# Attention result turned in 32x32 blocks on VectorE instead of transposed on TensorE, and the query and key weights loaded between the pieces of x

## The reference, cut to what matters

```python
xn = _layernorm(x)                       # x: (2, 1024, 256)
# attention: 16 heads of width 16, causal
q = einsum('btc,hcd->bhtd', xn, Wq) + bq;  k, v alike
probs = softmax(q @ k^T * 16**-0.5 + causal)
y = (probs @ v).transpose(0, 2, 1, 3).reshape(B, T, 256)
attn = y @ Wo + bo
# experts: 8, each token goes to its top 2
logits = xn @ Wr;  top2, softmax over the two
h_e = (clip(silu(xn @ Wg[e]), -7, 7) * (xn @ Wu[e])) @ Wd[e]
out = x + attn + sum over the two chosen e of gate * h_e
```

## Time and profile before

| | before |
|---|---|
| median of 3 runs | 441.28 us (441.12 to 441.63) |
| span of the profiled execution, first to last instruction | 440.0 us |
| around the span: median less span | 1.28 us |
| granted TensorE clock, mean over the span | 0.984 |
| busy: PE / DVE / ACT / POOL | 422.0 / 314.2 / 237.6 / 194.6 us |

### The profile page before, as it was taken

One profiled execution on the slowest core, in us unless ns is written; L12 is line 12 of the kernel. 1 busy time (PEld: TensorE's weight loads), 2 busy tenths in 40 slices (PEclk: granted clock), 3 DMA queues, 4 the chain that ended last, 5 costly groups with the idle time before them and its releaser, 6 DMA issues.

```text
span 440.0 us, 8430 instructions
## 1 busy us (share of the span) xinstructions
PE 422.0 (96%) x2851; PEld 255.2 (58%) x2851; DVE 314.2 (71%) x1019; ACT 237.6 (54%) x551; POOL 194.6 (44%) x223
## 2 busy tenths in 40 slices
PE   8898979989999999999999999999999999999896
PEld 8486425656364366557666676565655664756333
DVE  6827999999888835885577735867576768591485
ACT  1563363433647665655564546646555547464992
POOL 5331256585054277346744256233743365212410
PEclk9999959998999999999999999999999999999999
DMA  7289896788076249435784069621893454110582
GB/s 237 70 218 201 277 207 182 257 280 269 4 150 181 83 135 230 154 118 187 184 233 175 23 187 221 189 87 50 245 256 107 145 155 153 21 38 3 169 310 97
DMA packets 40373, 71.34 MB, mean 162 GB/s; under 512 B 5893, under 2 KB 30598, under 8 KB 40332
## 3 DMA queue, kind: packets, MB, share of 16 engines
q0 software_dynamic: 9360, 39.99, 28.8%
q1 hardware_dynamic: 27132, 26.76, 24.5%
q10 hardware_dynamic: 3840, 4.08, 3.6%
HBM read 55.85 MB, written 15.60 MB: 162 GB/s over the span
## 4 chain that ended last, share of the span: by engine, by line
PE 72%; DVE 18%; issue 3%; DMA 3%; POOL 2%; ACT 1%; SPq 0%; ACTq 0%
PE psum L1364 15%; PE psum L1307 14%; PE psum L1268 11%; PE psum L1287 11%; PE psum L1373 7%; DVE psum L1004 5%; DVE mxa L1007 5%; PE psum L1223 3%; PE psum L1199 3%; PE psum L1347 2%; DMA bqk<-in_bqk 2%; PE psum L1316 2%; PE psum L1354 2%; DVE resid L976 1%; POOL probs L823 1%
## 5 line engine op out<-in xcount | busy, mean ns | idle before, releaser
L896 ACT ACTIVATE probs<-psum 128x512 f32<-128x512 f32 (+1 forms) x320 | 151.5, 575 | 38.6 <-PE psum L1287 37.8
L1004 DVE CUSTOM_DVE_ANT_0 psum<-psum,maskrow 128x128 f32<-128x128 f32 (+3 forms) x256 | 121.4, 505 | 18.1 <-PE psum L1268 17.8
L1268 PE MATMUL psum<-packk,packq 96*128 96x512 bf16 (+3 forms) x384 | 93.3, 328 | 2.5 <-DVE mxa L1004 1.2
L1007 DVE TENSOR_REDUCE mxa<-psum 128x1 f32<-128x512 f32 x128 | 87.7, 685 | 9.4 <-PE psum L1268 9.2
L1287 PE MATMUL psum<-packq,packk 99*128 99x512 bf16 (+3 forms) x384 | 90.5, 332 | 2.9 <-ACT probs L896 2.7
L1307 PE MATMUL psum<-probs,v 128*32 128x512 f32 (+3 forms) x768 | 76.1, 502 | 2.2 <-POOL probs L823 1.8
L823 POOL TENSOR_SCALAR_AFFINE_SELECT probs<-probs 128x512 f32<-128x512 f32 (+1 forms) x48 | 40.0, 836 | 64.1 <-ACT probs L896 63.6
L1268 PEld LDWEIGHTS psum<-packk,packq 96*128 96x128 bf16 x384 | 34.5, 97 | 54.7 <-issue 16.8
L1287 PEld LDWEIGHTS psum<-packq,packk 99*128 99x128 bf16 x384 | 33.0, 98 | 45.1 <-issue 12.7
L790 POOL DMA_INDIRECT xg<-xn_rows,token x39 | 37.6, 965 | 45.9 <-PE psum L1354 35.9
L1166 DVE SCALAR_TENSOR_TENSOR tanh<-tanh,psum 128x256 f32<-128x256 f32 x39 | 16.3, 417 | 49.8 <-ACT tanh L931 49.5
(11 more groups left out here) (127 smaller groups left out, 477.2 us busy)
## 6 DMA issues: line engine op xcount, KB each, us to landing
qk_parts<-stage SPq DMA_DIRECT2D x24, 256.0 KB, 2.9
stage<-expert_rows SPq DMA_DIRECT2D x16, 256.0 KB, 4.1
packq<-qk_parts SPq DMA_DIRECT2D x16, 192.0 KB, 4.6
packk<-qk_parts SPq DMA_DIRECT2D x14, 192.0 KB, 6.1
x<-in_x SPq DMA_DIRECT2D x4, 512.0 KB, 5.3
packq<-qk_parts SPq DMA_DIRECT2D x16, 128.0 KB, 6.2
xn_rows<-probs ACTq DMA_DIRECT2D x4, 512.0 KB, 14.5
out<-x SPq DMA_DIRECT2D x16, 128.0 KB, 2.5
```

The costliest lines, as they stand in the source:

```text
L896: act.activation(probs[:, g % RING, h, 0:width], psum[:, bank, 0:width], ACT.Exp, scale=SCALE)\
L1004: ins = dve.tensor_tensor_reduce(out=chunk, in0=chunk, in1=maskrow[:, BANK - width:], scale=1.0, scalar=NEG, op0=ALU.add, op1=ALU.max, acc ...
L1007: ins = dve.tensor_reduce(into, chunk, op=ALU.max, axis=AX.X)
L1268: pe.matmul(psum[:, bank, 0:width], packq[0:MAXROW, u % SLOTS, i // HALF, h, P * (i % HALF):P * (i % HALF + 1)], packk[0:MAXROW, u % SLOTS ...
```

## The change

Two edits in one, with the plan made anew from them.

**The end of a half without TensorE.** DVE transposes the bank of `pv` in 32x32 blocks straight from PSUM to SBUF (`turn`). Block (h, b) holds head h and 32 tokens, so after it each partition is a token of one head, 16 values and the sum beside them. `normalise` takes the reciprocal and multiplies from SBUF to SBUF, into one half of the 32 columns of `ynorm`: even units into the first 16, odd units into the last 16. When both units of a pair are in, a second block transpose (`turn_back`) writes `yt` in the layout that the projection wants, with the features in another order, and `wo` and `bv` are laid out in that order on loading. The transposes of `y` on PE and the copies on ACT (`copy_y`, `copy_yt`, `copy_yt_half`) are gone. `ynorm` of the second half lies in the memory of `wvr`, free once the v tiles are done; the hot rows of the routing lie in `yt` now, and the widened v bias in the first slot of `xgt`, so the first gather waits for the bias product.

**The loads at the start.** SP issues x piece 0 and 1, then `wqk`, then x piece 2 and 3, then the value weights, `bv`, `wo`, `bo`. ACT issues only the bias `bqk`, without a wait, on a semaphore of its own, which ACT's first `hi` waits for in place of PE. The first matmul of a query/key tile waits only for the first 128 features of its piece. `WARM` is 52, not 60.

```diff
-WARM = 60
+WARM = 52
...
-        job("SP", ("x", q), 500, lag=2000, due=-10, size=524288)
-    job("ACT", ("weights_qk",), 950, [("SP", ("x", 1))], due=-50, lag=2000, size=540000)
-    job("ACT", ("weights_v",), 2200, [("ACT", ("weights_qk",))], due=-50, lag=2000, size=820000)
+        job("SP", ("x", q), 500, lag=2000, due=q - 10, size=524288)
+    job("SP", ("weights_qk",), 500, due=-8.5, lag=2000, size=524288)
+    job("ACT", ("bias_qk",), 2000, due=-60, lag=2000)
+    job("SP", ("weights_v",), 2000, due=-5, lag=2000, size=820000)
...
-            pe(("xnt", q, c), 436, [("DVE", ("ln", q))], due=10 * q, takes=("xnt", q, c))
+            pe(("xnt", q, c), 436, [("DVE", ("ln", q))], due=10 * q if q > 1 else q, takes=("xnt", q, c))
...
-        after = [("ACT", ("xnt", 2 * b + n, c)) for c in range(DC)] + [("ACT", ("weights_qk",))]
-        pe(("qk1", k), 853, after, due=due, takes=("qk", k))
-        pe(("qk2", k), 853, [("PE", ("qk1", k))], due=due - 1)
+        after = [("ACT", ("xnt", 2 * b + n, 0)), ("SP", ("weights_qk",))]
+        pe(("qk1", k), 853, after, due=due, takes=("qk", k), lag=0)
+        pe(("qk2", k), 853, [("PE", ("qk1", k)), ("ACT", ("xnt", 2 * b + n, 1))], due=due - 1)
...
-            job("ACT", ("y", u, c), 465, after, due - 1000, frees=("y", u, c))
-            pe(("y_t", u, c), 450, [("ACT", ("y", u, c))], due, ("y_t", u, c))
...
-            dve(("norm", u, c), 626, after, due, ("y_t", u, c))
+            dve(("turn", u, c), 640, [("PE", ("pv", g))], due - 1000, ("y", u, c))
+            dve(("norm", u, c), 900, [("DVE", ("turn", u, c)), ("PE", ("v", NT - 1))], due - 1000)
+            if u % 2:
+                after = [("DVE", ("norm", u - 1, c)), ("DVE", ("norm", u, c))]
+                if u == 1:
+                    after += [("PE", ("list",))]
+                if u > G:
+                    after += [("PE", ("proj", HALF * c + HALF - 1))]
+                dve(("back", u, c), 640, after, due)
...
-                    pe(("proj_t", t), 220 if t < LATE else 110, [("DVE", ("norm", u, c))], pdue, ("proj_t", t))
...
-                    job("ACT", ("yt", t), 252 if t < LATE else 200, after, pdue, frees=("proj_t", t))
-                    pe(("proj", t), 853 if t < LATE else 427, [("ACT", ("yt", t))], pdue, ("proj", t))
+                    pe(("proj", t), 853 if t < LATE else 427, [("DVE", ("back", u, c))], pdue, ("proj", t))
...
+            def turn(u, c):
+                bank = wait_filled(dve, ("y", u, c))
+                if u == c == 0:
+                    dve.wait_ge(ones_in, 16)
+                dve.transpose(yturn[:, :, :].rearrange("p a b -> p (a b)"), psum[:, bank, :]).then_inc(freed[bank], 1)
+
             def normalise(u, c):
-                bank = wait_filled(dve, ("y_t", u, c))
-                part = psum[:, bank, :].rearrange("p (t h w) -> p t h w", t=4, h=UH)
-                chain(rec_ready, dve.reciprocal(rec[:, :, :], part[:, :, :, HD]))
...
-                dve.tensor_tensor(dst, part[:, :, :, 0:HD], rec[:, :, :].unsqueeze(3).to_broadcast([P, 4, UH, HD]),
-                                  ALU.mult).then_inc(freed[bank], 1)
+                wait_freed(dve, ("y", u, c))
+                chain(rec_ready, dve.reciprocal(rec[:, :], yturn[:, :, HD]))
+                at = HD * (u % 2)
...
+                dve.tensor_tensor(ynorm[c][:, :, at:at + HD], yturn[:, :, 0:HD],
+                                  rec[:, :].unsqueeze(2).to_broadcast([P, BANK // QUAD, HD]), ALU.mult).then_inc(y_normal, 1)
+
+            def turn_back(u, c):
...
+                dve.wait_ge(y_normal, normals_before(u, c))
+                dve.transpose(yt[:, u % G // 2, BANK * c:BANK * (c + 1)],
+                              ynorm[c][:, :, :].rearrange("p a b -> p (a b)")).then_inc(y_back, 1)
...
+            def head_rows(t, c):
+                if t % HALF == 0:
+                    pe.wait_ge(y_back, backs_before(t, c))
+                return yt[:, c, P * (t % TB):P * (t % TB + 1)]
...
-            def transpose_y(u, c):
-            def transpose_heads(t):
-            def transpose_first_heads(t):
...
+    def head_order(w):
+        return np.moveaxis(w.reshape(DC, 2, UH, HD, -1), (2, 1, 3, 0), (0, 1, 2, 3)).reshape(P, DC, -1)
```

142 lines of the change are left out of this document (57 added, 85 removed).

## The result

The changed kernel takes 445.85 us (median of 4 runs, 445.62 to 446.2) against 441.45 us for the kernel before on the same chip: a ratio of 1.0086, 95% interval 1.0062 to 1.0109. It is slower, where I forecast 432.1 us. The profiled execution spans 443.9 us against 440.0, so 13.1 us are missing from the forecast span of 430.8. The other 0.6 us lie around the span (445.85 - 443.9 = 1.95, where I had put 1.3).

The account below looks back on a forecast made before the run. PE was taken as the bound from 120 to 400 us and DVE from 42 to 110. Terms -2.4 + 0.9 - 8.7 + 1.0 = -9.2 gave a span of 430.8, plus 1.3 makes 432.1 us; range 427.0 to 438.0.

Parts of the forecast that it names:

- the start: Loading and first query/key product: earlier bias and weights start it at 11.5 to 11.6 us, carried on; -2.4 us.
- the stretches that PE bounds: 120 to 432 us: 9.9 us of PE transposes go, 1.2 us of waits come back; -8.7 us.
- that row as a rival: ACT's queue stands 4.18 us in a DMA issue at 36.24; the start's gain is swallowed, 434.5 us; chance 0.11.
- The stretch that DVE bounds: 42 to 110 us: one block transpose, 0.65 us, and normalisations held by POOL, 0.25 us; +0.9 us.
- the 1.2 us put down for all waits together: 120 to 432 us: PE waits from 17 us more DVE work, taken against the 9.9 us removed.
- 0.25 us on 16: Each of 16 normalisations, now with both inputs in SBUF, held by POOL for 0.25 us on average.
- PE busy for 98% from 120 to 400 us: Sign for the PE-bound term: PE still busy 98% or more there, unit ends drifting ahead 1.2 us per unit.
- The end: After the last `pv`: expert sums before the reciprocal make the end 7.2 us instead of 6.2; +1.0 us.
- The rivals: PE work back as waits, 435.8 (0.20); start swallowed, 434.5 (0.11); more off, 428.5 (0.08); DVE the bound, 452 (0.05).
- The one on the slow side: DVE becomes the bound through 1.37 us block transposes and 0.8 us holds; 452 us with half exposed; chance 0.05.

Follow-up runs that it names:

- both_dues: The changed kernel with the due times and releases of the first transposes and query/key products as before; 441.45 us.
- load_dues: The kernel before with the start edit's loads, but the first transposes' and query/key products' due times and releases as before; 440.7 us.
- turn_only: The changed kernel with the start taken back (weights behind piece 1 on ACT's queue, 60 warming transposes), only the attention edit left; 440.66 us.
- load_only: The kernel before with the start edit alone (loads moved, bias apart, 52 warming transposes, second feature chunk awaited later); 445.63 us.
- light_before: The kernel before, order unchanged, with one PE transpose of each attention result instead of four; 439.34 us.
- rec_order: rec_psum's order of all engines, with the reciprocals in SBUF as in the changed kernel; 440.56 us.
- tail_first: The changed kernel with the last half's block transposes and normalisation given an earlier due time on DVE; 1.1 us off the end, total time not given.
- rec_psum: both_dues with the normalisation's reciprocals written into the freed PSUM bank, 268 of 993 PE steps standing elsewhere; 436.58 us.
- pool_order: load_only with seven GpSimd (POOL) steps put back in the order of the kernel before; 442.12 us.

## Why the prediction was wrong

Four terms of the sum failed, and the two large ones are the start (4.4 us of the 13.1) and the stretches that PE bounds (5.0). With the start right, the change would still have gained next to nothing: both_dues, with the old first order, took 441.45 us against 441.70 for the kernel before.

- **The start, -2.4: wrong in sign.** The first product came at 12.63 us, not at 11.6: the first piece of x landed 0.65 us later (statistics from 4.95 us, 4.30 before), and PE's order has both pieces' transposes, the second eight only at 11.70, ahead of it. Of this lead of 1.4 us 0.9 was left at the first v product, and none at the routing. The step that failed is "the stores, loads, v tiles, routing and the DVE chain from 42 us on hang on it": at 37 us they hang on ACT's stalled issue, and the order there decides what PE and DVE have done by then. I had named that row as a rival and priced it at the loss of the 2.4. Against the forecast it cost 4.4 by the routing: 2.4 lost and 2.0 more, by a wait of 2.35 us (0.9 longer than before) and a clock at half behind it. load_dues, with the same loads and the old first order, was 1.85 us early at the routing: the transfers' part of the term was nearly right, the order's was not in it.
- **The stretch that DVE bounds, +0.9: measured +1.9** from the routing to unit 1 (2.0 to 3.8). The block transpose was right, 0.71 against 0.65 us. The held instructions were not those I priced: POOL's steps moved beside the small ones of the maxima. turn_only, with the same transpose, was 1.9 us early at unit 1; the loss is the start edit's. So for the attention edit alone the term had the wrong sign in these two executions (-1.8, not +0.9), and for the start edit it had nothing, where load_only lost 2.2 us in this stretch. POOL's order had no part in the prediction.
- **The stretches that PE bounds, -8.7: measured -3.7** behind unit 1's first score. Seven tenths of the work removed come off (light_before), so by my estimate some -7 of -9.9 (0.7 x 9.9). The step that failed is the 1.2 us put down for all waits together: in rec_order one hold of 2.15 us cost 3.5, and the changed kernel has the same hold of 2.16 at 175.6 us. It has a second loss at 274 us: tail_first, in the same order, goes by there with a PE wait of 0.97 us instead of 1.45 and a granted clock of 1.00 instead of 0.57, and gains 1.3 us on it. Without any hold rec_psum reached -5.7. These parts come from different orders and don't add up to the -3.7 exactly. I spread the holds as 0.25 us on 16; they came as 2.16, 0.32, 0.26 and 0.14, a mean of 0.18, which is not far off. The cost is not in the mean. The sign that I had named for this term, PE busy for 98% from 120 to 400 us, came (274.61 of 280) and the gain did not: a busy share tells neither the clock nor the short waits.
- **The end, +1.0: measured +3.7.** The order of the steps was as I had read it. DVE came free 0.8 us after the last `pv`, where I had put nothing, and the eight products took 3.75 us where I had put 1.7: I took the pace of a PE that has just worked, for a PE that had stood 5.8 us.
- **The rivals.** No rival reached 445.9 by its mechanism. The one on the slow side wanted DVE to become the bound; it was busy 76% from 120 to 400 us. The kernel is slower, for which I gave a chance of 0.05, by causes that no rival named; what a new order costs by itself was in none of them.

Not settled: why the clock falls behind some waits and not behind others. It fell behind 1.45 us at 274 us in the changed kernel, and stayed up behind 2.16 us at 99 us there and behind 2.39 us in pool_order. The wait at 274 us (ACT's copy waits 4.43 us for a scatter to land, PE 1.45 us for that copy) was not taken away by an experiment. Keeping PE at work at 37 us was not tried.

## What to carry to other kernels

Where a planner writes the order, an edit's own cost and the cost of the order it brings must be forecast and tested apart: keep the old order with the new transfers first. Read every engine's new order, the least busy one too, around the places where another engine is the bound. Whether a lead is carried past a stall depends on the work that the order has ahead of it: load_dues kept 1.85 of its 2.0 us, load_only none of its 1.6. And a new wait of microseconds on PE must be priced with the work behind it at half the clock as well.
